# Key norms as two products of 64 rows, and the front of the feed-forward part inside the end of the attention loop

## The chip, the cores and the metric

The kernel runs on one core of one Trainium2 chip. The metric is the device time of one execution in microseconds (us); lower is better. TensorE is called PE here (PEld for its weight loads), VectorE DVE, ScalarE ACT, GpSimd POOL, and the queue that issues the transfers SP.

## The reference

A block of a transformer over 8 sequences of 512 tokens with 256 channels. Cut to what matters:

```python
x = x + _layernorm(attn(_layernorm(x)))          # 16 heads of 64 complex channels
x = x + _layernorm(ffn(_layernorm(x)))           # hidden size 768, silu(gate) * up, int weights / 127

# in attn, for each head (q, k, v are complex, rotated by a phase that depends on the token):
s  = einsum('bihd,bjhd->bhij', qr, conj(kr)).real
qn = (q.real ** 2 + q.imag ** 2).sum(-1)          # norm of each query
kn = (k.real ** 2 + k.imag ** 2).sum(-1)          # norm of each key
maha   = maximum(qn[..., None] + E*E * kn[:, :, None, :] - 2.0 * E * s, 0.0) / V
logits = coef * log1p(maha / nu) - 0.5 * DH * log(V)      # then causal mask and softmax
y      = A @ v                                            # and the output projection Wo
```

E depends on the distance of the two tokens and on the head. The causal mask makes a head's scores a triangle: of four blocks of 128 queries the widest sees 512 keys, then 384, 256 and 128.

## The kernel before

The attention runs as 64 iterations: 8 groups of two heads (the outer loop, `G`), and in each group the 8 sequences (`B`). Iteration t works on the scores and logits of unit t (one sequence, two heads), while it projects and rotates unit t+1 and finishes unit t-1 (its softmax weights are turned and multiplied with the values, and the result goes through the output projection). In `body` of every engine `c` stands for unit t, `cn` for t+1 and `cp` for t-1; `if nxt` and `if old` leave out what has no next or no former unit.

Each engine has its own program, written out by hand, and it takes its instructions strictly in that order. Semaphores tie the engines together: `x.wait_ge(sem, v)` stops an engine (and all that stands behind it) until the count is there. The two PSUM banks `pa` hold projections and norms, `ps` the scores, `pp` turned weights and values, `py` the weighted values, `po` the output projection.

Steps by name, for head `hh` of the unit and block `n` (0 is the widest, 512 columns, 3 the narrowest, 128):

- PE: `project` (6 products of 512 columns), `norm_k` and `norm_q`, `scores`, `turn` (transposes), `attend`, `values`, `out_project`.
- ACT: `square`, `keep_norm_k` (norms of the keys into `kn`), `log`, `exp`, `keep_turned`, `keep_y`, `keep_values`. Log and exp lie in different tables, so ACT loads a table (1.28 us) four times an iteration.
- DVE: `rotate` (8 of them), `decay`, `distance`, `logits`, `bounds`, `inverse`, `add_output` (adds into `acc`).
- POOL: `rotated` (8 of them, 64 x 512), `sum_squares`, `decay_norm` (writes `ek`, which `distance` reads), and once a group `low_weights`.

The squares in `sq` have the 64 channels of head 0 in rows 0 to 63 and those of head 1 in rows 64 to 127. `norm_k` (L710 to 714) multiplies all 128 rows with a matrix `heads[:, hh, :]` that is one in the rows of head hh and zero in the others, and so spreads the norms of one head over 128 partitions; it is called once for each head. All this is 32-bit data, for which one product shows as two MATMUL records.

After the 64 iterations comes the run-out of the last unit, then the feed-forward part, one sequence after the other. For sequence b: `first_norm` (statistics of the attention's sum), `residual` (normalise, add the input, statistics again), `second_move`, `f_normal` on ACT, `f_transposes` on PE, `f_high` and `split_low` (the input as a high and a low part), then six times `gate_up` (PE), `silu` (ACT), `hidden` (DVE, L1577), `hidden_high` (ACT), `hidden_low` (POOL, L635), then `down` (PE), `third_norm`, `third_move`, `f_last` (ACT) and `f_final` (DVE). `f_pow` (POOL, L640) stands between each statistics step and its use. All of the feed-forward part's front for sequence 0 waits for the last `add_output` of the attention: `dve.wait_ge(acc_dve, 4 * B * G + 4)`.

## Time and profile before

| | |
|---|---|
| median of 3 runs | 2025.73 us (2020.53 to 2025.87) |
| the profiled execution | 2020.74 us, its span 2018.9 us |
| busy: PE, DVE, ACT, POOL | 91%, 80%, 78%, 71% of the span |
| share of POOL in the chain that ended last | 49% |

The busy time of PE counts a product until its modelled end, so that a busy PE is not one at its peak. "Idle before" is the time that an engine sat still just before an instruction, with what ended it. The chain that ended last is followed back from the last instruction: it says what released what, not how much slack the other engines had.

### The profile page before, as it was taken

What the parts mean: (1) busy time and instruction counts of PE and PEld (TensorE: products, weight loads), DVE (VectorE), ACT (ScalarE), POOL (GpSimd) and SP (SyncE); (2) the same over time, 40 slices, a digit from 0 to 9 for tenths busy, and PEclk for the clock granted to TensorE, in tenths of its full rate; (3) what the DMA queues carried; (4) which work ended last, traced back from release to release, by engine and by line L of the source; (5) the groups of instructions that cost most, each with busy time, mean ns of one, the idle gap of its engine ahead of it and who ended that gap; (6) DMA issues with size and microseconds to landing.
All of it is one profiled execution on the core that took longest, in us unless ns stands there. A gap on an engine that the chain in (4) does not pass through costs nothing.

```text
span 2018.9 us, 41149 instructions
## 1 busy us (share of the span) xinstructions
PE 1845.1 (91%) x10660; PEld 1512.1 (75%) x10660; DVE 1605.3 (80%) x3834; ACT 1566.9 (78%) x3217; POOL 1440.2 (71%) x1257
## 2 busy tenths in 40 slices
PE   0489999999999999999999999999999999968886
PEld 0358878887878788878787888788888888856665
DVE  5458888888888888888888888888888888865774
ACT  2758888888888888888888888888888888864444
POOL 1377887778777878787778777887778777724443
PEclk9999999999999999999999999999999999999999
DMA  8813111311131113111311131111311110110110
GB/s 178 295 61 105 57 43 43 105 42 37 43 107 42 58 43 105 42 58 43 88 41 58 43 99 49 57 43 56 92 42 43 43 35 33 39 32 11 50 45 32
DMA packets 65069, 128.17 MB, mean 63 GB/s; under 512 B 14448, under 2 KB 44656, under 8 KB 55920
## 3 DMA queue, kind: packets, MB, share of 16 engines
q1 hardware_dynamic: 64880, 126.01, 20.4%
q8 instruction: 75, 1.23, 0.3%
q14 instruction: 114, 0.93, 0.1%
HBM read 107.24 MB, written 25.03 MB: 66 GB/s over the span
## 4 chain that ended last, share of the span: by engine, by line
POOL 49%; issue 23%; PE 12%; DVE 7%; ACT 3%; SPq 2%; POOLq 2%; DMA 1%; ACTq 0%; DVEq 0%
POOL qk L567 27%; POOL ek L576 16%; POOL sq L559 5%; PE pa L705 2%; PE py L766 2%; PE ps L742 2%; PE po L777 2%; DVE stats L1517 1%; PE pp L732 1%; PE pp L754 1%; DVE tabs L1577 1%; POOL rstd L640 1%; PE pa L714 1%; SPq L436 1%; DMA xs_d<-xt 1%
## 5 line engine op out<-in xcount | busy, mean ns | idle before, releaser
L567 POOL TENSOR_TENSOR qk<-rm 64x512 f32<-64x512 f32 x512 | 671.6, 1312 | 83.8 <-DVE rm L1351 23.7
L576 POOL TENSOR_TENSOR ek<-tabs,kn 128x512 f32<-128x512 f32 (+3 forms) x512 | 476.4, 936 | 259.3 <-DVE lg L1376 228.9
L705 PE MATMUL pa<-xt,wt 128*128 128x512 f32 x1536 | 438.2, 421 | 5.0 <-issue 2.6
L1384 DVE CUSTOM_DVE_ANT_0 lg<-lg,tabs,ncog 128x512 f32<-128x512 f32 (+3 forms) x512 | 428.1, 845 | 0.0
L1351 DVE TENSOR_TENSOR rm<-pa,tabs 128x512 f32<-128x512 f32 x512 | 337.6, 680 | 45.0 <-POOL qk L567 36.5
L742 PE MATMUL ps<-qk 128*128 128x512 f32 (+3 forms) x1024 | 351.4, 443 | 20.4 <-DVE lg L1376 18.0
L766 PEld LDWEIGHTS py<-pt,vt 128*128 128x128 f32 x2560 | 343.0, 191 | 27.6 <-ACT pt L1060 4.7
L766 PE MATMUL py<-pt,vt 128*128 128x128 f32 x2560 | 353.7, 276 | 2.5 <-ACT pt L1060 2.1
L1376 DVE CUSTOM_DVE_ANT_0 lg<-ps,ek,qb 128x512 f32<-128x512 f32 (+3 forms) x512 | 278.7, 544 | 75.5 <-DVE ps L1365 57.7
L705 PEld LDWEIGHTS pa<-xt,wt 128*128 128x128 f32 x1536 | 280.4, 189 | 72.4 <-issue 7.4
L1053 ACT ACTIVATE pr<-lg,nmax 128x512 f32<-128x512 f32 (+3 forms) x512 | 285.5, 558 | 56.3 <-DVE nmax L1384 46.7
L1405 DVE SCALAR_TENSOR_TENSOR acc<-po,rden,acc 128x256 f32<-128x256 f32 (+1 forms) x512 | 223.4, 477 | 109.4 <-PE po L777 109.3
L1060 ACT ACTIVATE pt<-pp 128x512 f32<-128x512 f32 (+3 forms) x512 | 212.4, 428 | 123.3 <-PE pp L754 118.1
L777 PE MATMUL po<-wot,yt 128*128 128x256 f32 x1024 | 268.9, 385 | 2.9 <-DVE acc L1405 2.5
L1045 ACT ACTIVATE lg<-lg,qb 128x512 f32<-128x512 f32 (+3 forms) x512 | 264.9, 556 | 6.6 <-DVE ncog L1480 3.4
L1365 DVE TENSOR_TENSOR ps<-ps,tabs 128x512 f32<-128x512 f32 (+3 forms) x512 | 251.2, 491 | 11.5 <-issue 5.5
L754 PEld LDWEIGHTS pp<-ident,pr 128*128 128x128 f32 x1280 | 164.2, 141 | 109.4 <-issue 100.9
L742 PEld LDWEIGHTS ps<-qk 128*128 128x128 f32 x1024 | 171.8, 189 | 98.0 <-DVE lg L1376 52.8
L754 PE MATMUL pp<-ident,pr 128*128 128x128 f32 x1280 | 223.3, 273 | 0.8 <-ACT pt L1060 0.8
L732 PE MATMUL pp<-wt,xt 128*128 128x256 f32 x1536 | 199.3, 286 | 0.0
L777 PEld LDWEIGHTS po<-wot,yt 128*128 128x128 f32 x1024 | 175.0, 190 | 17.5 <-DVE acc L1405 2.2
L732 PEld LDWEIGHTS pp<-wt,xt 128*128 128x128 f32 x1536 | 187.8, 191 | 0.1
(152 smaller groups left out, 2193.4 us busy)
## 6 DMA issues: line engine op xcount, KB each, us to landing
xt<-xs_d SPq DMA_DIRECT2D x62, 1024.0 KB, 4.8
tabs<-vec_d SPq DMA_DIRECT2D x64, 192.0 KB, 4.9
xs_d<-xt SPq DMA_DIRECT2D x8, 1024.0 KB, 5.8
wt<-wraw_d SPq DMA_DIRECT2D x8, 768.0 KB, 7.6
acc<-in_L_attn_x SPq DMA_DIRECT2D x8, 512.0 KB, 7.5
tabs<-rope_d SPq DMA_DIRECT2D x16, 256.0 KB, 5.5
tabs<-in_L_attn_x SPq DMA_DIRECT2D x8, 512.0 KB, 4.6
out<-tabs SPq DMA_DIRECT2D x8, 512.0 KB, 3.0
```

The source lines that it names most:

```text
L567: pool.tensor_tensor(qk[part * DH:(part + 1) * DH, z * HH + hh, :], rm[row, 2 * part, :], rm[row, 2 * part + 1, :], ALU.add if part else A ...
L576: pool.tensor_tensor(ek[:, n % 2, 0:w], tab(par, hh, E2_T, N - w), kn[:, hh, 0:w], ALU.mult).then_inc(ek_pool, 1)
L705: last = mm(pa[r][:, :], wproj(par, z, kt, a, r * P, (r + 1) * P), xt[slot][:, kt, b, :], start=(n == 0), stop=(n == 3 * KT - 1))
L732: last = mm(pp[half][:, jj * W2:(jj + 1) * W2], xt[slot][:, kt, a, j * P:(j + 1) * P], wproj(par, 2, kt, b, 0, W2), start=(n == 0), stop=( ...
L742: mm(ps[n % 2][:, 0:w], qk[:, hh, TILES[n] * P:(TILES[n] + 1) * P], qk[:, HH + hh, 0:w], start=True, stop=True).then_inc(s_rdy, 1)
L754: last = pe.transpose(pp[i][:, j * P:(j + 1) * P], pr[:, hh, o:o + P], ident[:, :])
L766: last = mm(py[:, I * P:(I + 1) * P], vt[:, slot, j, hh * P:(hh + 1) * P], pt[:, i, j * P:(j + 1) * P], start=(j == 0), stop=(j == I))
L777: last = mm(po[:, jj * D:(jj + 1) * D], yt[:, hh, j * P:(j + 1) * P], wot[:, par, hh * D:(hh + 1) * D], start=True, stop=True)
L1053: act.activation(pr[:, hh, at(n)], lg[:, hh, at(n)], ACT.Exp, bias=nmax[:, q:q + 1], scale=-1.0, accum_out=den[:, q:q + 1]).then_inc(ex_ac ...
L1351: tt(rm[:, m, :], pa[r][:, :], ropet(par, m in (IS, RS)), ALU.mult).then_inc(mul_dve, 1)
L1376: dve._custom_dve(bass.dve_ops.TENSOR_ADD_SAT, out=lg[:, hh, at(n)], in0=ps[n % 2][:, 0:w], in1=ek[:, n % 2, 0:w], s0=3e38, s1=qb[:, slot, ...
L1384: dve.tensor_tensor_reduce(lg[:, hh, at(n)], lg[:, hh, at(n)], tab(par, hh, T3_T, N - w), ncog[:, par, 0, hh:hh + 1], 3e38, ALU.add, ALU.m ...
```

## The change

Two things, and an order of all four engines' programs written anew around them.

1. `norm_k`, called twice with 128 rows, becomes `norms_k`, called once: for each head a product of only that head's 64 rows, one directly behind the other. The semaphore `nk_rdy` now counts one per unit.
2. The front of the feed-forward part for sequences 0 and 1 (`first_norm`, `residual`, `second_move`, `f_normal`, `f_transposes`, `f_high`, `split_low` and the first two `gate_up` of sequence 0) moves into the last iteration (`if not nxt`) and into the run-out. For it `f_xin` lies wholly in `tabs[0]`, which the last group does not use, and the transposes of sequence 0 go to `pa` instead of `pp`. SP loads the inputs a group earlier.
3. In the loop `decay`, `distance` and `scores` of blocks 0 to 2 of head 0 are done one iteration earlier, `decay_norm` too, and `sum_squares` stands ahead of `rotated`. In the feed-forward part of the other sequences `residual(b + 1)` moves ahead of `hidden(b, 0)`, `f_final` behind `second_move`, and `split_low` ahead of `third_move`.

```diff
-        f_xin = [seq(0, 0), seq(1, 0)]
-        f_outs = [seq(0, 2), seq(1, 2)]
+        f_xin = [seq(0, 0), seq(0, 2)]
+        f_outs = [seq(1, 0), seq(1, 2)]
...
-            sp.wait_ge(f_dve, 8 * B * G + 8)
-            sp.wait_ge(ek_pool, 8 * B * G + 8)
+            sp.wait_ge(f_dve, 8 * B * (G - 1) + 8)
...
-            def rotated(c, z, hh, part):
+            def rotated(c, z, hh, part, last=False):
...
+                if not last:
+                    pool.wait_ge(rot_pool[hh], c[4] + 2 * z + part + 1)
...
+                pool.wait_ge(rot_pool[1], c[4] + 4)
...
-                decay_norm(c, 0, 2, it.par)
                 decay_norm(c, 0, 3, it.par)
...
-                if nxt:
-                    pool.wait_ge(ek_pool, c[8] + 5)
+                if not nxt:
+                    f_pow(0, 0)
+                if nxt:
+                    sum_squares(cn, 0)
+                    pool.wait_ge(sum_pool, cn[2] + 1)
                     rotated(cn, 0, 0, 0)
                 decay_norm(c, 1, 1, it.par)
                 if nxt:
-                    sum_squares(cn, 0)
+                    pool.wait_ge(ek_pool, c[8] + 6)
+                    rotated(cn, 0, 0, 1)
                 decay_norm(c, 1, 2, it.par)
+                if not nxt:
+                    f_pow(1, 0)
                 if nxt:
                     pool.wait_ge(ek_pool, c[8] + 7)
-                    rotated(cn, 0, 0, 1)
                     rotated(cn, 0, 1, 0)
                     rotated(cn, 0, 1, 1)
                     sum_squares(cn, 1)
-                decay_norm(c, 1, 3, it.par)
-                if nxt:
-                    pool.wait_ge(ek_pool, c[8] + 8)
+                    pool.wait_ge(sum_pool, cn[2] + 2)
                     rotated(cn, 1, 1, 0)
                     rotated(cn, 1, 0, 0)
                     rotated(cn, 1, 0, 1)
-                    rotated(cn, 1, 1, 1)
+                decay_norm(c, 1, 3, it.par)
+                if not nxt:
+                    f_pow(0, 1)
+                if nxt:
                     decay_norm(cn, 0, 0, it.behind)
+                    decay_norm(cn, 0, 1, it.behind)
+                    decay_norm(cn, 0, 2, it.behind)
+                    pool.wait_ge(ek_pool, cn[8] + 3)
+                    rotated(cn, 1, 1, 1, True)
             pool.wait_ge(grp[0], 16 * TABLE_LOADS)
             c0 = counts(pool, 0, PERS)
...
-            def norm_k(c, hh):
+            def norms_k(c):
                 pe.wait_ge(sum_pool, c[2] + 2)
-                pe.wait_ge(mul_dve, c[8] + 7 + hh)
-                mm(pa[hh][:, :], heads[:, hh, :], sq[:, 1, 0, :], start=True, stop=True).then_inc(nk_rdy, 1)
+                pe.wait_ge(mul_dve, c[8] + 8)
+                for hh in range(HH):
+                    row = slice(hh * DH, (hh + 1) * DH)
+                    last = mm(pa[hh][:, :], heads[row, hh, :], sq[row, 1, 0, :], start=True, stop=True)
+                last.then_inc(nk_rdy, 1)
...
                 pe.wait_ge(f_norm, b + 1)
+                dst = pp if b else pa
+                if b == 0:
+                    pe.wait_ge(qb_dve, B * G + 1)
+                    pe.wait_ge(kn_act, 2 * B * G + 2)
+                if b == 1:
+                    pe.wait_ge(pt_act, 8 * B * G + 8)
                 for kt in range(KT):
...
+                if n0 == 0:
+                    pe.wait_ge(x_dve, 8 * B * G + 8)
...
+                if not nxt:
+                    f_transposes(0)
+                if nxt:
+                    norms_k(cn)
+                if old:
+                    out_project(cp, it.before, 1, 0)
+                if nxt:
+                    scores(cn, 0, 0)
+                    norm_q(cn)
+                    scores(cn, 0, 1)
+                if old:
+                    out_project(cp, it.before, 1, 1)
+                turn(c, 0, 1)
+                if nxt:
...
+            turn(c, 1, 3)
+            gate_up(0, 1)
+            out_project(c, 1, 0, 0)
+            attend(c, 1, 1, 1)
+            attend(c, 1, 2, 1)
+            attend(c, 1, 3, 1)
+            out_project(c, 1, 0, 1)
+            out_project(c, 1, 1, 0)
+            out_project(c, 1, 1, 1)
+            gate_up(0, 2)
+            gate_up(0, 3)
+            f_transposes(1)
+            gate_up(0, 4)
+            gate_up(0, 5)
...
+            keep_turned(c, 1, 2)
+            silu(0, 0)
+            keep_turned(c, 1, 3)
+            silu(0, 1)
+            keep_y(c, 1)
+            f_normal(1)
+            hidden_high(0, 0)
+            silu(0, 2)
+            hidden_high(0, 1)
+            silu(0, 3)
...
-                hidden_high(b, 3)
                 if b + 1 < B:
                     f_high(b + 1)
+                hidden_high(b, 3)
                 silu(b, 4)
                 hidden_high(b, 4)
                 silu(b, 5)
                 hidden_high(b, 5)
...
-                distance(c, 0, 1, it.slot)
+                decay(c, 0, 3, it.par)
+                distance(c, 0, 3, it.slot)
+                if old:
+                    logits(cp, 1, 3, it.before)
+                if not nxt:
+                    dve.wait_ge(acc_dve, 4 * (B * G - B + 1) + 4)
+                    first_norm(0)
...
+                    inverse(cp, 0)
+                if nxt:
                     rotate(cn, it.behind, 0, RS)
                     rotate(cn, it.behind, 0, IC)
...
+                    residual(0)
+                decay(c, 1, 2, it.par)
+                if nxt:
+                    rotate(cn, it.behind, 1, RC)
+                distance(c, 1, 2, it.slot)
                 if old:
                     add_output(cp, it.b_before, 0, 0)
-                logits(c, 0, 1, it.par)
-                decay(c, 1, 2, it.par)
-                logits(c, 0, 2, it.par)
-                if nxt:
-                    rotate(cn, it.behind, 1, RC)
+                if nxt:
                     rotate(cn, it.behind, 1, IS)
+                logits(c, 1, 0, it.par)
...
+                if old:
+                    add_output(cp, it.b_before, 0, 1)
+                if not nxt:
+                    first_norm(1)
                 decay(c, 1, 3, it.par)
                 distance(c, 1, 3, it.slot)
...
             c = counts(dve, G * B - 1, PERS)
-            logits(c, 1, 0, 1)
-            logits(c, 1, 1, 1)
-            logits(c, 1, 2, 1)
             logits(c, 1, 3, 1)
             inverse(c, 0)
+            split_low(0)
             add_output(c, B - 1, 0, 0)
             inverse(c, 1)
+            residual(1)
             add_output(c, B - 1, 0, 1)
+            hidden(0, 0)
             add_output(c, B - 1, 1, 0)
             add_output(c, B - 1, 1, 1)
...
+            second_move(1)
             dve.wait_ge(acc_dve, 4 * B * G + 4)
-            first_norm(0)
-            residual(0)
-            second_move(0)
-            first_norm(1)
-            split_low(0)
-            for b in range(B):
+            hidden(0, 1)
+            hidden(0, 2)
+            hidden(0, 3)
+            split_low(1)
+            hidden(0, 4)
+            first_norm(2)
+            hidden(0, 5)
+            for b in range(1, B):
+                if b + 1 < B:
+                    residual(b + 1)
                 hidden(b, 0)
+                if b + 1 < B:
+                    second_move(b + 1)
                 if b >= 2:
                     f_final(b - 2)
-                if b + 1 < B:
-                    residual(b + 1)
                 hidden(b, 1)
-                if b + 1 < B:
-                    second_move(b + 1)
                 hidden(b, 2)
-                if b >= 1:
-                    third_norm(b - 1)
+                third_norm(b - 1)
                 hidden(b, 3)
-                if b >= 1:
-                    third_move(b - 1)
                 if b + 1 < B:
                     split_low(b + 1)
+                third_move(b - 1)
                 hidden(b, 4)
                 if b + 2 < B:
                     first_norm(b + 2)
```

What the diff leaves out: in the loop the order of the other steps on ACT and PE, and the functions of the feed-forward part, which only moved up in the file.

PE, the end of the last iteration but one, in the order of the loop, before (`pp` from `xt` are the values, L714 the key norms, `pp` from `pr` the turns, L721 the query norms, `po` the output projection, `ps` the scores):

```order
L732 MATMUL pp<-wt,xt 128x256 x24
L777 MATMUL po<-wot,yt 128x256 x2
L766 MATMUL py<-pt,vt 128x128
L714 MATMUL pa<-sq,heads 128x512
L754 MATMUL pp<-ident,pr 128x128 x4
L777 MATMUL po<-wot,yt 128x256 x2
L714 MATMUL pa<-sq,heads 128x512
L754 MATMUL pp<-ident,pr 128x128 x3
L721 MATMUL pa<-heads,sq 128x2 x4
L777 MATMUL po<-wot,yt 128x256 x2
L742 MATMUL ps<-qk 128x512
L742 MATMUL ps<-qk 128x384
```

PE, the same place in the changed kernel (L735 the key norms):

```order
L754 MATMUL pp<-wt,xt 128x256 x24
L788 MATMUL py<-pt,vt 128x128
L799 MATMUL po<-wot,yt 128x256 x2
L776 MATMUL pp<-ident,pr 128x128 x4
L735 MATMUL pa<-sq,heads 128x512 x2
L799 MATMUL po<-wot,yt 128x256 x2
L764 MATMUL ps<-qk 128x512
L743 MATMUL pa<-heads,sq 128x2 x4
L764 MATMUL ps<-qk 128x384
L799 MATMUL po<-wot,yt 128x256 x2
L776 MATMUL pp<-ident,pr 128x128 x3
L764 MATMUL ps<-qk 128x256
```

The two products of the key norms now follow each other with nothing between, and scores of three blocks stand behind them, not of two.

DVE, the feed-forward part of one sequence in the middle, before (L1577 is `hidden`, L1563 `f_final`, L1539 the sum in `residual`, L1517 statistics, L1529 the shifts):

```order
L1517 BN_STATS stats<-acc 128x6 x4
L1521 BN_AGGR mv<-stats 128x2 x4
L1524 TENSOR_SCALAR rstd<-mv 128x4
L1577 SCALAR_TENSOR_TENSOR tabs<-ps,tabs 128x512 x2
L1563 TENSOR_TENSOR tabs<-tabs,acc 128x1024
L1529 SCALAR_TENSOR_TENSOR xshift<-mv,rstd 128x4
L1539 SCALAR_TENSOR_TENSOR acc<-acc,rstd,tabs 128x256 x4
L1517 BN_STATS stats<-acc 128x6 x4
L1521 BN_AGGR mv<-stats 128x2 x4
L1524 TENSOR_SCALAR rstd<-mv 128x4
L1577 SCALAR_TENSOR_TENSOR tabs<-ps,tabs 128x512
```

DVE, the same place in the changed kernel (L1521 is `hidden`, L1507 `f_final`, L1483 the sum in `residual`):

```order
L1461 BN_STATS stats<-acc 128x6 x4
L1465 BN_AGGR mv<-stats 128x2 x4
L1468 TENSOR_SCALAR rstd<-mv 128x4
L1521 SCALAR_TENSOR_TENSOR tabs<-ps,tabs 128x512
L1473 SCALAR_TENSOR_TENSOR xshift<-mv,rstd 128x4
L1483 SCALAR_TENSOR_TENSOR acc<-acc,rstd,tabs 128x256 x4
L1461 BN_STATS stats<-acc 128x6 x4
L1465 BN_AGGR mv<-stats 128x2 x4
L1468 TENSOR_SCALAR rstd<-mv 128x4
L1521 SCALAR_TENSOR_TENSOR tabs<-ps,tabs 128x512
L1473 SCALAR_TENSOR_TENSOR xshift<-mv,rstd 128x4
L1507 TENSOR_TENSOR tabs<-tabs,acc 128x1024
```

`residual` of the next sequence moved ahead of `hidden(b, 0)`; before, `hidden(b, 0)` and `f_final` stood in front of it.

DVE, the run-out of the attention, before (L1405 is `add_output`):

```order
L1384 ISA lg,nmax<-lg,tabs,ncog 128x128
L1384 ISA nmax 128x1
L1390 RECIPROCAL rden<-den 128x4
L1405 SCALAR_TENSOR_TENSOR acc<-po,rden,acc 128x256 x2
L1390 RECIPROCAL rden<-den 128x4
L1405 SCALAR_TENSOR_TENSOR acc<-po,rden,acc 128x256 x6
L1517 BN_STATS stats<-acc 128x6 x4
L1521 BN_AGGR mv<-stats 128x2 x4
L1524 TENSOR_SCALAR rstd<-mv 128x4
```

DVE, the run-out in the changed kernel (L1455 is `add_output`, L1513 `split_low`, L1521 `hidden`):

```order
L1440 RECIPROCAL rden<-den 128x4
L1513 TENSOR_TENSOR xt<-pa,xt 128x512 x2
L1455 SCALAR_TENSOR_TENSOR acc<-po,rden,acc 128x256 x2
L1440 RECIPROCAL rden<-den 128x4
L1473 SCALAR_TENSOR_TENSOR xshift<-mv,rstd 128x4
L1483 SCALAR_TENSOR_TENSOR acc<-acc,rstd,tabs 128x256 x4
L1461 BN_STATS stats<-acc 128x6 x4
L1465 BN_AGGR mv<-stats 128x2 x4
L1468 TENSOR_SCALAR rstd<-mv 128x4
L1455 SCALAR_TENSOR_TENSOR acc<-po,rden,acc 128x256 x2
L1521 SCALAR_TENSOR_TENSOR tabs<-ps,tabs 128x512
L1455 SCALAR_TENSOR_TENSOR acc<-po,rden,acc 128x256 x4
```

The whole of `residual(1)` stands between the first and the second `add_output` of the last unit, and `hidden(0, 0)` between the second and the third.

## Rows read from the trace of the kernel before

**Rows 1.** The page: the chain that ended last by engine, and its largest group.

```profile
POOL 49%; issue 23%; PE 12%; DVE 7%; ACT 3%; SPq 2%; POOLq 2%; DMA 1%; ACTq 0%; DVEq 0%
...
L567 POOL TENSOR_TENSOR qk<-rm 64x512 f32<-64x512 f32 x512 | 671.6, 1312 | 83.8 <-DVE rm L1351 23.7
```

**Rows 2.** Busy PE, PEld, DVE, ACT, POOL, clock, DMA: one iteration, then one feed-forward sequence.

```profile
626.00:652.00 26.00, 25.91 (x155) 21.49 (x154) 22.14 (x54) 22.19 (x47) 20.51 (x19) 1.00 0.12 40
1890.00:1914.00 24.00, 19.27 (x108) 15.27 (x107) 16.39 (x45) 11.58 (x24) 10.97 (x9) 1.00 0.14 44
```

**Rows 3.** Who waited for whom, 626 to 652: total, times, longest.

```profile
POOL ek L576 <- DVE lg L1376: 3.9, 3, 1.7
...
PEld ps L742 <- DVE lg L1376: 0.5, 2, 0.3
```

**Rows 4.** PE in order of time: start, length, line, count; the query norms of four iterations.

```profile
139.34 1.02 PE L721 MATMUL pa<-heads,sq 128*128 128x2 f32 x8
...
666.59 0.95 PE L721 MATMUL pa<-heads,sq 128*128 128x2 f32 x8
...
695.51 0.95 PE L721 MATMUL pa<-heads,sq 128*128 128x2 f32 x8
...
1769.20 0.95 PE L721 MATMUL pa<-heads,sq 128*128 128x2 f32 x8
```

**Rows 5.** PE in order of time, around the second product of the key norms.

```profile
639.61 1.02 PE L714 MATMUL pa<-sq,heads 128*128 128x512 f32 x2
640.47 0.49 PE L754 MATMUL pp<-ident,pr 128*128 128x128 f32 x3
640.79 0.95 PE L721 MATMUL pa<-heads,sq 128*128 128x2 f32 x8
```

**Rows 6.** One line, L721: records, shortest, median and longest in ns.

```profile
L721 PE MATMUL pa<-heads,sq x512: 170/251/352, 117.6 to 1769.9; 128*128 128x2 f32 x171
```

**Rows 7.** DVE and PE in order of time, end of attention, feed-forward front.

```profile
1806.71 0.88 DVE L1405 SCALAR_TENSOR_TENSOR acc<-po,rden,acc 128x256 f32<-128x256 f32 x2 [1.22 <-PE po L777]
...
1818.03 1.97 PE L889 MATMUL pp<-ident,tabs 128*128 128x128 f32 x8 [11.35 <-ACT tabs L1161]
1821.50 2.04 PE L903 MATMUL pa<-xt,wgt 128*128 128x512 f32 x4 [1.50 <-DVE xt L1569]
...
1841.53 0.68 DVE L1577 SCALAR_TENSOR_TENSOR tabs<-ps,tabs 128x512 f32<-128x512 f32 x1
...
1862.52 0.68 DVE L1577 SCALAR_TENSOR_TENSOR tabs<-ps,tabs 128x512 f32<-128x512 f32 x1
```

**Rows 8.** DVE, POOL, ACT and PE in order of time, a feed-forward sequence in the middle.

```profile
1886.42 0.68 DVE L1577 SCALAR_TENSOR_TENSOR tabs<-ps,tabs 128x512 f32<-128x512 f32 x1
...
1893.02 1.66 DVE L1539 SCALAR_TENSOR_TENSOR acc<-acc,rstd,tabs 128x256 f32<-128x256 f32 x4
...
1896.81 1.01 POOL L640 TENSOR_TENSOR rstd<-rstd,mhalf 128x4 f32<-128x4 f32 x1 [3.74 <-DVE rstd L1524]
...
1898.06 2.07 ACT L1161 ACTIVATE tabs<-acc,xshift,rstd 128x256 f32<-128x256 f32 x4 [6.59 <-DVE xshift L1529]
...
1889.16 0.74 PE L919 MATMUL py<-wdt,wt 128*128 128x256 f32 x4 [0.80 <-POOL wt L635]
...
1896.86 1.09 PE L903 MATMUL pa<-xt,wgt 128*128 128x512 f32 x4
...
1901.77 0.75 DVE L1517 BATCH_NORM_STATS2 stats<-py 128x6 f32<-128x256 f32 x2
...
1903.82 0.68 DVE L1577 SCALAR_TENSOR_TENSOR tabs<-ps,tabs 128x512 f32<-128x512 f32 x1
...
1910.30 0.68 DVE L1577 SCALAR_TENSOR_TENSOR tabs<-ps,tabs 128x512 f32<-128x512 f32 x1
```

**Rows 9.** DVE in order of time: `logits` of 256 columns at two places of an iteration.

```profile
632.72 1.16 DVE L1384 CUSTOM_DVE_ANT_0 lg<-lg,tabs,ncog 128x256 f32<-128x256 f32 x1
...
648.32 0.47 DVE L1384 CUSTOM_DVE_ANT_0 lg<-lg,tabs,ncog 128x256 f32<-128x256 f32 x1
```

592 lines of the change are left out of this document (291 added, 301 removed).

## The prediction

> **What bounds the kernel now.** I read the page first. It seems to say POOL: the chain that ended last runs through POOL for 49% of the span, and PE, though busy for 91% of the span, takes only 12% of it [rows 1]. But that chain only says who released whom. So I cut out one iteration in the middle (626 to 652 us) and looked at the busy time of each engine: PE 25.91 of 26.00, ACT 22.19, DVE 22.14, POOL 20.51 [rows 2]. Only PE is full. The waits of the same stretch agree: POOL sat 3.9 us waiting for DVE, while PE's weight loads waited only 0.5 us [rows 3]. A busy PE is not yet a PE at its peak, so I looked at how closely its work is packed. The second product of the key norms starts at 639.61 and the turns behind it at 640.47, those at 640.79 give way to the query norms [rows 5]: each begins where the last one's stream ends. The iteration is bound by PE's stream; it repeats from one query norm to the next in 25.80 us (640.79 to 666.59) [rows 4, 5]. The iteration of a group in which POOL splits weights takes 28.92 (666.59 to 695.51), and over all 62 steps from 139.34 to 1769.20 the mean is 26.29 [rows 4].
>
> Behind the loop another limit holds. The last `add_output` ends at 1807.6; PE then idles 11.35 us for the normalised input and 1.50 more for the split, and its first gate products run at 1821.50 in 2.04 us where later ones take 1.09 [rows 7, 8]: the pause has cost it the clock too. `hidden(0, 5)` ends at 1842.2, 34.6 us behind the last sum, `hidden(1, 5)` at 1863.2 [rows 7]. From then on a sequence takes 23.88 us (1886.42 to 1910.30) in which no engine is full: PE 19.27, DVE 16.39, ACT 11.58 of 24.00 [rows 2, 8]. That is a chain of latencies across engines.
>
> **Key norms.** Two records of 512 columns take 0.86 us (639.61 to 640.47), so 0.43 each, and the two heads 1.72 us an iteration [rows 5]. A product of 64 rows is no shorter: it streams the same 512 columns. A gain comes only if products in different rows of the array run side by side. The four records come in the order A1 A2 B1 B2 (A is head 0). A2 needs A's rows again, B1 doesn't: at best A2 and B1 run together, three slots of 0.43 in place of four, 0.43 us saved. If each head's two passes paired with the other's (A1 with B1, A2 with B2), it would be 0.86. The trace of before has no product on 64 rows, so it shows neither. The bound below: nothing overlaps, and the array must run empty before it changes between 128 and 64 rows and once more behind it. The shortest record, a product of 2 columns, takes 170 ns [rows 6]; streaming 2 columns is next to nothing of that, so I take it as the price of one emptying, and lose 0.34 us. So the term is between +0.34 and -0.86; I take -0.43, since it follows from the order of the records with no further condition. Over 63 iterations: 27 us less, and 21 more to 54 less at the bounds.
>
> The Trainium skill bears on both ends. "TensorE: Matmul & The Clock Gate", Part 3, says that products in different row groups start about 4 ns apart and run concurrently; by it the 27 us come. "TensorEngine Tiling (Array Packing)", Key Properties, says that changing the tiling mode drains the array, which speaks against this change; by it some of the gain is given back each iteration. No row here shows either.
>
> **The loop's new order.** Since PE is full, a new order can gain at most PE's waits, 0.5 us, and I count nothing for it. It can lose. I laid the steps of the new order on PE's stream, with 25.37 us for an iteration, and asked for each step who must be done before it. The tightest places are these. `scores(cn, 0, 2)` ends PE's iteration and needs `distance` of block 0, one `decay`, `bounds` and one `distance` after `scores(cn, 0, 0)`: about 0.7 us to spare. `turn(cp, 1, 3)` needs `exp` of block 3 of head 1, which comes behind a table load of 1.28: 0.7 to spare. `rotate(cn, 1, RC)` waits for `rotated` of head 1, which now must wait for `scores(c, 1, 3)`; DVE sits there, and ends its rotations 1.2 us before the key norms want them. `decay_norm(c, 0, 3)` now stands behind the last `rotated` at the iteration's edge, and is done 0.6 us before `distance`. POOL's program has the same 8 rotations, 8 `decay_norm` and 2 sums, 20.51 us, DVE's and ACT's the same work as before [rows 2]: 3 us of room in each. The weight split (28.92 in place of 25.80) stays at the start of POOL's iteration, and `decay_norm` of blocks 3 and 4 wait for it where blocks 1 to 3 did: no change.
>
> **The front inside the end.** Before, 34.6 us lie between the last sum and `hidden(0, 5)`. Now at the last sum the normalised input, both parts of it, two `gate_up` and `hidden(0, 0)` of sequence 0 are done. What is late next is sequence 1: `second_move(1)` stands on DVE behind the last `add_output`, and ACT, which takes its program in order, has `f_normal(1)` ahead of `hidden_high(0, 0)`. So from the last sum on, the time is that from a `f_normal` to a `hidden(b, 5)`: 1898.06 to 1910.98, 12.9 us, less 2.05 for the third statistics (1901.77 to 1903.82), which sequence 0 hasn't [rows 8], plus 0.2 for `second_move`: 11.1. That is 23.5 less. But the last sum is itself later, since the new work lies in the way: two `gate_up` on PE ahead of `out_project(1, 0, 0)` (four groups of 1.09 less the tail of 0.17 that the next one hides, 3.7 [rows 6, 8]), the transposes of sequence 0 (1.0, and about 1.8 waiting for ACT's `f_normal(0)`, itself behind DVE's `residual(0)`), and `residual(1)` between the first and second `add_output`, 3.8 (1893.02 to 1896.81 [rows 8]). Sum 10.3, of which it fills about 1.4 in which PE waited anyway: 8.9 later. Net 14.6 us. SP's loads are no obstacle: they wait for counts of the group before.
>
> **The later sequences.** Count from the end of `hidden(b-1, 5)` (1887.10). Before: `hidden(b, 0)`, `f_final` and `residual` bring POOL's power at 1896.81, which takes 1.01, ACT's `f_normal` starts at 1898.06 and holds ACT for 2.07, and only behind it come `hidden_high(b, 1)`, `silu(b, 2)` and `hidden(b, 2)`, so the third statistics start at 1901.77, 14.7 us behind [rows 8]. Now `residual` starts at once: 3.8, power 1.0, `f_normal` done by +7.5. The third statistics then wait for PE: `down` starts at 1889.16 (+2.1), two `down` and the `gate_up` between them end at 1896.86 (+9.8), and I take +10.0 [rows 8]. Before it, 9.2 us follow to the end of `hidden(b, 5)` (1901.77 to 1910.98) [rows 8]; these are left as they are. New period 19.2 in place of 23.88, 4.7 less, for five sequences 23.4. Sequence 1 had no `f_final` to wait for and took 21.0 (1842.2 to 1863.2): 1.8 less. Sequence 7 has no `residual`: nothing. Sum 25.2. The cover here is PE's own `down`: even if POOL's `hidden_low(b-1, 5)`, which now runs beside `residual`, held it up for 2 us, `f_normal` would end at +9.5, still under 10.
>
> **Sum.** 27 + 14.6 + 25.2 = 66.8 us. The profiled execution took 2020.74 (span 2018.9): 1954 by this sum. It is the lower end of the three runs shown (2020.53 to 2025.87), the median is 5 higher: 1959. I say 1957.
>
> **Rivals.**
> (1) The norms don't gain: no overlap, or the array's emptying eats it (three slots and 0.34 of emptying leave 0.09 us an iteration, 6 in all; four slots lose up to 21). The key norms' start-to-start would stay at 1.6 to 2.0 us. For it: nothing in the trace shows an overlap. The 40 us behind the loop remain: 1979 to 2000, with 1984 for no effect. The page on tiling, above, is the rule that would do this.
> (2) Full pairing, 0.86: 54 + 40 us, 1929. Against it: the records of one head stand behind each other.
> (3) Slower: the loop changes hands to the chain DVE, POOL, PE. From `scores(c, 1, 3)` POOL does five rotations of 1.31 and a sum, about 8 us [rows 1], PE the scores, 1 us, then DVE somewhat over half of its 22.14 [rows 2], `decay`, `distance`, `logits` and `rotate`, until `distance(c, 1, 1)` lets the next `scores(c, 1, 3)` go: some 22 us, with hand-overs 23. A `logits` of 256 columns took 1.16 us at one place and 0.47 at another; the long one ran beside POOL's work [rows 9]. If such losses of 0.7 us hit four more of DVE's steps, the period would pass 25.8, and at 26.5 it eats the 40 us of the feed-forward part: 63 x 0.7 = 44, so 2025 and above. It decides from 1.1 us of new stall per iteration on.
> (4) The feed-forward part gives half: `residual(1)` and the transposes block the end more, or `hidden_high` comes later than laid out: 20 in place of 40 us, 1977 with the norms' gain.
>
> **Chances.** Forecast as summed (1943 to 1972) 0.5; (1) 0.2; (2) 0.1; (4) 0.1; (3) or anything else that takes all of it 0.1. The likeliest is 1957. For 8 in 10 I leave out the upper part of (1) and all of (3): 1928 to 1990. A measurement here tells about 0.3% (6 us) from no change. Faster by over 0.3%: 0.9; within: 0.03; slower: 0.07.
>
> **What would show it.** Key norms: the first record of `norms_k` to the next instruction's start in 1.3 us, not 1.7, with one record starting while the other still runs. Loop: query norm to query norm in 25.4, PE still above 25.2 busy of it, and no wait of PE over 0.5. End: last `add_output` to `hidden(0, 5)` in 11, no pause of PE over 3 us, the first gate products in 1.1. Later: `hidden(b, 5)` every 19.2. It is wrong if a product of 64 rows brings stalls of its own, or if PE starts to wait for DVE in the loop.

## The result, and the profile after

| | median us | runs |
|---|---|---|
| before | 2024.38 | 2020.53 to 2025.87 |
| changed | 1975.59 | 1970.88 to 1978.42 |

The ratio is 0.976, with a 95% interval of 0.9735 to 0.9784: 49 us faster, where 67 were forecast. The profiled execution of the changed kernel took 1975.62 us (span 1973.8). Its trace can be cut at the same marks as that of before. The query norm L743 (formerly L721) marks the iterations, in order of time on PE; columns are start, length, line, count:

```profile
147.47 0.95 PE L743 MATMUL pa<-heads,sq 128*128 128x2 f32 x8
...
668.25 0.95 PE L743 MATMUL pa<-heads,sq 128*128 128x2 f32 x8
...
698.47 0.95 PE L743 MATMUL pa<-heads,sq 128*128 128x2 f32 x8
```

The first one in the loop is 8.1 us later than before (139.34, [rows 4]). Of this, 5.1 come with the order (in `order_only`, below, it is at 144.46), for the other 3.0 see the last section. The last starts at 1759.21, so 62 steps took 1611.7 us, 18.1 less than before. An ordinary step takes 25.12 (643.13 to 668.25, for one), where it took 25.80 and I expected 25.37; one that splits weights takes 30.22 (above, 668.25 to 698.47), where it took 28.92 [rows 4] and I expected no more. The busy times of the stretch of [rows 2], and of one feed-forward sequence:

```profile
626.00:652.00 26.00, 26.00 (x157) 21.16 (x156) 22.95 (x56) 22.90 (x48) 21.36 (x20) 1.00 0.11 40
...
1861.80:1880.74 18.94, 17.92 (x106) 15.39 (x104) 16.23 (x45) 11.55 (x22) 11.85 (x10) 1.00 0.19 56
```

PE is full in the loop as before, and now nearly full in the feed-forward part too. The key norms, on PE in order of time; the last two rows are the same four records seen through narrower windows, two that start at 1731.22 and two at 1731.73:

```profile
1730.60 0.60 PE L776 MATMUL pp<-ident,pr 128*128 128x128 f32 x4
1731.22 1.13 PE L735 MATMUL pa<-sq,heads 64*128 64x512 f32 x4
1732.28 1.13 PE L799 MATMUL po<-wot,yt 128*128 128x256 f32 x4
...
1731.22 0.70 PE L735 MATMUL pa<-sq,heads 64*128 64x512 f32 x2
...
1731.73 0.62 PE L735 MATMUL pa<-sq,heads 64*128 64x512 f32 x2
```

Four records from first start to next instruction: 1.06 us. By [rows 5] they took 0.86 twice. The end, on DVE and ACT:

```profile
1802.38 0.88 DVE L1455 SCALAR_TENSOR_TENSOR acc<-po,rden,acc 128x256 f32<-128x256 f32 x2 [9.16 <-PE po L799]
...
1812.14 0.88 DVE L1455 SCALAR_TENSOR_TENSOR acc<-po,rden,acc 128x256 f32<-128x256 f32 x2 [2.17 <-PE po L799]
...
1813.12 2.08 ACT L1111 ACTIVATE tabs<-acc,xshift,rstd 128x256 f32<-128x256 f32 x4 [8.56 <-DVE xshift L1473]
...
1823.26 0.68 DVE L1521 SCALAR_TENSOR_TENSOR tabs<-ps,tabs 128x512 f32<-128x512 f32 x1
...
1842.19 0.68 DVE L1521 SCALAR_TENSOR_TENSOR tabs<-ps,tabs 128x512 f32<-128x512 f32 x1
```

From the last `add_output` (ends 1813.0) to the end of `hidden(0, 5)` (1823.9) it is 10.9 us, against 34.6 in [rows 7]; but from the last query norm of the loop to that last sum it is 53.8, against 38.4. Later sequences follow each other every 18.9 us, against 23.9 in [rows 8].

What stands behind the last query norm of the loop takes 214.6 us instead of 249.7: 35 less, where 40 were forecast. The loop, where 27 us were forecast from the norms, gave 18 in its 62 steps, but 8 had been lost ahead of them: 10 in all. Together this is 45, the difference of the two spans. The experiments take the change apart. All were timed beside the kernel before, whose median lay between 2024.7 and 2025.9 in them.

### The profile page after: what moved, and what is told of

It is laid out like the page before. It is cut to its first block and busy times, and to the rows that moved or that the text cites. A ratio compares the mean times of both kernels' runs of the same rounds, so it can differ in the third digit from the quotient of the medians.

```text
span 1973.8 us, 41342 instructions
## 1 busy us (share of the span) xinstructions
PE 1815.5 (92%) x10660; PEld 1491.2 (76%) x10660; DVE 1601.2 (81%) x3834; ACT 1577.3 (80%) x3217; POOL 1460.0 (74%) x1257
## 5 line engine op out<-in xcount | busy, mean ns | idle before, releaser
L567 POOL TENSOR_TENSOR qk<-rm 64x512 f32<-64x512 f32 x512 | 693.7, 1355 | 110.9 <-PE ps L764 50.0
L577 POOL TENSOR_TENSOR ek<-tabs,kn 128x512 f32<-128x512 f32 (+3 forms) x512 | 462.8, 910 | 145.1 <-DVE lg L1426 100.3
L1434 DVE CUSTOM_DVE_ANT_0 lg<-lg,tabs,ncog 128x512 f32<-128x512 f32 (+3 forms) x512 | 437.0, 872 | 0.0
L764 PE MATMUL ps<-qk 128*128 128x512 f32 (+3 forms) x1024 | 375.7, 451 | 8.9 <-DVE lg L1426 6.2
L788 PEld LDWEIGHTS py<-pt,vt 128*128 128x128 f32 x2560 | 333.8, 193 | 17.0 <-issue 0.3
L724 PEld LDWEIGHTS pa<-xt,wt 128*128 128x128 f32 x1536 | 287.5, 195 | 71.9 <-issue 14.1
L1082 ACT ACTIVATE lg<-lg,qb 128x512 f32<-128x512 f32 (+3 forms) x512 | 278.8, 558 | 35.5 <-DVE lg L1426 31.6
L1455 DVE SCALAR_TENSOR_TENSOR acc<-po,rden,acc 128x256 f32<-128x256 f32 (+1 forms) x512 | 221.9, 474 | 19.8 <-PE po L799 18.4
L776 PE MATMUL pp<-ident,pr 128*128 128x128 f32 x1280 | 215.3, 275 | 20.4 <-ACT pt L1097 16.3
L1065 ACT ACTIVATE sq<-pa 128x512 f32<-128x512 f32 x256 | 151.8, 593 | 88.2 <-PE pa L724 88.2
L559 POOL TENSOR_TENSOR sq<-sq 128x512 f32<-128x512 f32 x128 | 164.9, 1288 | 63.9 <-ACT sq L1065 63.8
```

The source lines that it names most:

```text
L567: pool.tensor_tensor(qk[part * DH:(part + 1) * DH, z * HH + hh, :], rm[row, 2 * part, :], rm[row, 2 * part + 1, :], ALU.add if part else A ...
L577: pool.tensor_tensor(ek[:, n % 2, 0:w], tab(par, hh, E2_T, N - w), kn[:, hh, 0:w], ALU.mult).then_inc(ek_pool, 1)
L724: last = mm(pa[r][:, :], wproj(par, z, kt, a, r * P, (r + 1) * P), xt[slot][:, kt, b, :], start=(n == 0), stop=(n == 3 * KT - 1))
L764: mm(ps[n % 2][:, 0:w], qk[:, hh, TILES[n] * P:(TILES[n] + 1) * P], qk[:, HH + hh, 0:w], start=True, stop=True).then_inc(s_rdy, 1)
L776: last = pe.transpose(pp[i][:, j * P:(j + 1) * P], pr[:, hh, o:o + P], ident[:, :])
L788: last = mm(py[:, I * P:(I + 1) * P], vt[:, slot, j, hh * P:(hh + 1) * P], pt[:, i, j * P:(j + 1) * P], start=(j == 0), stop=(j == I))
```

## Experiments

### The norms, in the new order and in the old

`norms_full` undoes the norms alone:

```diff
-                    row = slice(hh * DH, (hh + 1) * DH)
-                    last = mm(pa[hh][:, :], heads[row, hh, :], sq[row, 1, 0, :], start=True, stop=True)
+                    last = mm(pa[hh][:, :], heads[:, hh, :], sq[:, 1, 0, :], start=True, stop=True)
```

> The changed kernel with the key norms back as two products of 128 rows, at the same place. Theory: 0.48 us per iteration come back, 64 times: 2006. Rival (in the new order other engines set the pace as soon as TensorE has slack, so the norms are worth less): 1976 to 1990.

Measured 2010.59 us, ratio to before 0.9934 (0.9918 to 0.9951). The norms are worth 35.0 us in the new order. Its ordinary step is 25.72 us: 0.60 more than 25.12, which is more than my theory's 0.48. PE, in order of time:

```profile
671.56 0.60 PE L775 MATMUL pp<-ident,pr 128*128 128x128 f32 x4
672.05 1.98 PE L734 MATMUL pa<-sq,heads 128*128 128x512 f32 x4
673.87 1.03 PE L798 MATMUL po<-wot,yt 128*128 128x256 f32 x4
```

From the turns to the output product it is 2.31 us here and 1.68 with 64 rows (1730.60 to 1732.28, above). Joined, the four records of 128 rows take 1.82, a little more than 0.86 twice.

`same_rows` lets both heads' products read the same 64 rows:

```diff
-                    row = slice(hh * DH, (hh + 1) * DH)
-                    last = mm(pa[hh][:, :], heads[row, hh, :], sq[row, 1, 0, :], start=True, stop=True)
+                    row = slice(0, DH)
+                    last = mm(pa[hh][:, :], heads[row, 0, :], sq[row, 1, 0, :], start=True, stop=True)
```

> The changed kernel with the second head's norm product reading the first head's 64 rows as well (so the second head's key norms are those of the first). Theory (the gain is two heads in different rows at once): the four records run one after another at 0.43, 1.72 instead of 1.06, plus 0.66 x 64 = 42: 2018. Rival (a product of 64 rows is cheaper by itself): no change, 1976.

Measured 2030.78 us, 1.0022 (1.001 to 1.0035): 55 us slower than the changed kernel, and slower than the norms of 128 rows by 20. The rows, the last three from moments of the same product:

```profile
683.85 0.60 PE L776 MATMUL pp<-ident,pr 128*128 128x128 f32 x4
684.38 1.98 PE L735 MATMUL pa<-sq,heads 64*128 64x512 f32 x4
686.29 1.13 PE L799 MATMUL po<-wot,yt 128*128 128x256 f32 x4
...
684.91 0.59 PE L735 MATMUL pa<-sq,heads 64*128 64x512 f32 x1
...
685.34 0.59 PE L735 MATMUL pa<-sq,heads 64*128 64x512 f32 x1
...
685.77 0.59 PE L735 MATMUL pa<-sq,heads 64*128 64x512 f32 x1
```

Here the records start one after another, 0.43 apart from the second on. With different rows they run two and two. The rival, that a product of 64 rows is cheaper by itself, is out. And the full pairing is there. I had ruled it out by the order A1 A2 B1 B2, which I took from how the products are written. Since records of the same rows don't run together, each pair must hold one record of either head. The rows show also what changing between 128 and 64 rows can cost when nothing is paired: 2.44 us from turns to output product against 2.31, so at most 0.13 (the step is 25.96 against 25.72, 0.24 longer; the other 0.11 I can't place). "TensorEngine Tiling (Array Packing)" of the Trainium skill, Key Properties, says such a change drains the array; the 0.13 agrees with it, and is far less than the 0.34 of my bound.

`norms_alone` is the kernel before with the new norms, both behind the first turn:

```diff
-                if nxt:
-                    norm_k(cn, 0)
                 turn(c, 0, 0)
+                if nxt:
+                    norms_k(cn)
                 if old:
                     out_project(cp, it.before, 1, 0)
-                if nxt:
-                    norm_k(cn, 1)
                 turn(c, 0, 1)
```

> The kernel before with one edit: the key norms as two 64-row products, standing after the first turn. Theory (in the trace of after the four records run in two pairs, 1.06 us from first start to the next work, and about 0.18 is lost ahead of them, against 1.72 before): 0.48 us per iteration, 64 times, so 31 us faster than before, 1994. My prediction's pairing of the middle two records only: 0.43 x 64 = 27, 1997. Rival: in the old order another chain than TensorE's decides, and little of it reaches the end: 2015 to 2025.

Measured 2063.84 us, 1.0195 (1.0178 to 1.0212): slower, by 39 us, which neither theory nor rival expected. An ordinary step grew from 25.80 to 26.44. PE in order of time:

```profile
655.90 1.13 PE L716 MATMUL pa<-sq,heads 64*128 64x512 f32 x4 [1.02 <-DVE rm L1351]
```

The two products go into both buffers `pa`, so `norms_k` waits for the last rotary product, `rotate(cn, 1, IC)`, that reads the second of them. Before, the first norm needed only the one ahead of it, and the turn and an output product lay between. The old DVE order has that last product late. `norms_rotate` moves it, and nothing else:

```diff
                 if nxt:
                     rotate(cn, it.behind, 1, RS)
+                    rotate(cn, it.behind, 1, IC)
                 decay(c, 1, 3, it.par)
                 distance(c, 1, 3, it.slot)
                 if old:
                     add_output(cp, it.b_before, 0, 1)
-                if nxt:
-                    rotate(cn, it.behind, 1, IC)
```

> The kernel with the norms alone (old order, 2063.8 us, an iteration every 26.44, TensorE waits 1.0 there for the last rotary product of VectorE) with that one product moved two steps ahead on VectorE, before the last decay product. Theory: that wait is the whole loss; it goes, and the 0.6 of the shorter norms shows: an iteration every 25.2, 78 us faster, 1986. Rival: the product cannot come much sooner, since it waits for GpSimd's rotation and its halves must be ready, and the iteration stays over 26: 2030 or more.

Measured 2003.74 us, 0.9893 (0.9877 to 0.991): 60 us faster than `norms_alone`. The wait is gone, as the rows show, and the ordinary step is 25.52.

```profile
654.52 0.49 PE L745 MATMUL ps<-qk 128*128 128x128 f32 x2 [0.19 <-DVE lg L1376]
...
661.29 1.13 PE L716 MATMUL pa<-sq,heads 64*128 64x512 f32 x4
```

It lies between theory and rival. In the old order the new norms with this move are worth 22 us, 0.28 a step, and not the 0.6 of the new order. The move with the old norms was not tried, so how much of the 22 it gives by itself is not shown. The 0.19 above is a wait of PE that the stretch [rows 2] does not have; what the other 0.1 is stays open. The norms and the order are not two independent terms: the same change of the norms costs 39 us in the old order, brings 22 together with the moved rotary product, and brings 35 in the new order.

### The order by itself

`order_only` undoes the three other parts at once: norms of 128 rows, `f_transposes(0)`, `gate_up(0, 0)` and their kin behind the attention part, and the old order of sequences 1 to 7. The two products of the norms stay one behind the other.

> The changed kernel with its three other parts undone: norms of 128 rows, the front behind the attention part, the old order of sequences 1 to 7. What is left is the new order of the loop. Theory by the sum of what the others were worth in the new order (35 for the norms and 5.5 for the front, measured; 25 for the later sequences, predicted): 1976 + 65 = 2041, so the order alone costs about 17 us. The trace of after says where: the iteration that splits the weights takes 30 to 31.4 us instead of 28.7, and the first one 5 more. Rival, as the prediction counted it: the order alone is worth nothing, 2024.

Measured 2042.67 us, 1.0091 (1.0074 to 1.0108): the order alone costs 17.5 us. By the two profiled executions, whose spans differ by 19.6 us, the cost lies in three places. The seven steps that split the weights take 30.8 to 31.3 us (before 28.3 to 28.9), 16.4 more in all. The first query norm in the loop comes 5.1 later. The two steps at which the outer loop jumps back (last section) take 62.9 us, before 57.3: 5.6 more. The other 53 steps give 4.3 of it back (an ordinary one is 25.72, before 25.80), and what stands behind the last query norm gives 3.3.

Together the four parts add up: 35.0 for the norms, 5.5 for the front and 25.0 for the later sequences (below), less 17.5, make 48.0; the whole change gave 48.8.

What happens in such a step of the changed kernel, on ACT, POOL and DVE:

```profile
672.73 1.47 ACT L349 ACTIVATE wt<-wt 128x1536 fp32r<-128x1536 f32 x1
...
674.28 3.44 POOL L354 TENSOR_TENSOR wt<-wt 128x1536 fp32r<-128x1536 f32 x1 [1.49 <-ACT wt L349]
677.69 1.67 POOL L577 TENSOR_TENSOR ek<-tabs,kn 128x128 f32<-128x128 f32 x2
...
678.49 0.35 DVE L1426 CUSTOM_DVE_ANT_0 lg<-ps,ek,qb 128x128 f32<-128x128 f32 x1 [4.60 <-POOL ek L577]
```

POOL comes to the split at its iteration's start, waits 1.49 us for ACT's half, works 3.44, and only then makes the decay table of block 3, for which DVE sits idle 4.60 us; and behind DVE wait `log`, the turns and PE. In the kernel before, DVE did not wait for POOL there at all. First `logits(cp, 1, 0)` and `logits(cp, 1, 1)` in an ordinary step, then POOL's split and the same two beside it:

```profile
645.75 0.97 DVE L1384 CUSTOM_DVE_ANT_0 lg<-lg,tabs,ncog 128x512 f32<-128x512 f32 x1
...
646.65 0.61 DVE L1384 CUSTOM_DVE_ANT_0 lg<-lg,tabs,ncog 128x384 f32<-128x384 f32 x1
...
670.57 3.49 POOL L354 TENSOR_TENSOR wt<-wt 128x1536 fp32r<-128x1536 f32 x1 [0.80 <-ACT wt L349]
...
671.60 3.00 DVE L1384 CUSTOM_DVE_ANT_0 lg<-lg,tabs,ncog 128x512 f32<-128x512 f32 x1
...
674.53 1.34 DVE L1384 CUSTOM_DVE_ANT_0 lg<-lg,tabs,ncog 128x384 f32<-128x384 f32 x1
...
675.80 0.62 DVE L1376 CUSTOM_DVE_ANT_0 lg<-ps,ek,qb 128x384 f32<-128x384 f32 x1
```

The two took 2.76 us longer beside the split, most of the 3.1 us that this step lost before, and the `distance` behind them (L1376) then started without a wait. In all seven such steps the wide one took 3.0 to 3.3 us. That POOL's work is what slows them fits the traces, as in [rows 9], but was not tried apart.

`split_spread` cuts POOL's part in four pieces (2, 1, 1 and 2 sixths; the five in what I expected is a miscount) and puts them where POOL waits, in this step and the next, which `it.new == -1` marks. PE needs the weights only in the one after. Three of the four:

```diff
-                if it.raw is not None:
-                    low_weights(pool, 1 - it.par, it.ready)
...
+                if isinstance(it.new, int) and it.new == -1:
+                    low_weights(pool, 1 - it.par, it.ready, 2, 3)
                 if nxt:
                     sum_squares(cn, 0)
...
+                    if it.raw is not None:
+                        low_weights(pool, 1 - it.par, it.ready, 0, 2)
+                    if isinstance(it.new, int) and it.new == -1:
+                        low_weights(pool, 1 - it.par, it.ready, 4, 6)
                     decay_norm(cn, 0, 2, it.behind)
```

> The changed kernel with the weight split on GpSimd cut into 5 pieces that stand behind the work VectorE waits for, in that iteration and the next. Theory: the 4.6 us that VectorE waits for the decay table behind the split goes; the iteration takes about 26.5 instead of 30.7, seven times: 29 us faster, 1947. Rival: it is ScalarE's half of the split (1.5 us at the start of its iteration) that costs, and GpSimd's is hidden: 1976 to 1970.

Measured 1943.75 us, 0.9598 (0.9582 to 0.9614): 31.8 us faster than the changed kernel. The two steps that hold pieces now take 25.3 to 25.9 each. POOL in order of time shows a piece without a wait on either side:

```profile
682.65 1.27 POOL L356 TENSOR_TENSOR wt<-wt 128x512 fp32r<-128x512 f32 x1
683.89 0.73 POOL L581 TENSOR_TENSOR ek<-tabs,kn 128x256 f32<-128x256 f32 x1
```

### The feed-forward part

`front_back` puts the front for sequences 0 and 1 behind the last sum (`f_transposes(0)`, `gate_up(0, 0)` and `gate_up(0, 1)` behind the output products, `f_normal(0)`, `f_high(0)` and the first `silu` behind `keep_y`, the norms, `residual` and `second_move` behind the sums, with the powers on POOL).

> The changed kernel with the front of the feed-forward part for sequences 0 and 1 put back behind the attention part. By the trace of after the front inside the run-out saves 23.7 us behind the last sum and makes the last sum about 15 us later, so about 8 us come back: 1984. By the prediction's terms (23.5 and 8.9) 14.6 come back: 1990. Rival: the added waits of the last iteration eat all of it, 1976 or less.

Measured 1981.06 us, 0.9784 (0.9768 to 0.9801): the front gives 5.5 us. By the two traces, from the last query norm of the loop to the last sum it is 40.6 us with the front behind and 53.8 with it inside, 13.2 later where I forecast 8.9. From there to the end of `hidden(0, 5)` it is 29.7 and 10.9.

`residual_late` takes the old order of sequences 1 to 7 on POOL, ACT and DVE. Its core, on DVE:

```diff
-                if b + 1 < B:
-                    residual(b + 1)
                 hidden(b, 0)
-                if b + 1 < B:
-                    second_move(b + 1)
                 if b >= 2:
                     f_final(b - 2)
+                if b + 1 < B:
+                    residual(b + 1)
                 hidden(b, 1)
+                if b + 1 < B:
+                    second_move(b + 1)
                 hidden(b, 2)
```

> The changed kernel with the old order of sequences 1 to 7 in the feed-forward part (the residual of the next sequence behind the first hidden product and the store, second move behind the second, rstd and split back in their places). Theory: the period of a sequence goes from 18.9 back to 23.9, 25 us slower: 2001. Rival: the pool, vector and scalar parts of the old order matter less behind the new front, under 15 us: 1985.

Measured 2000.62 us, 0.9873 (0.9857 to 0.989): 25.0 us, and `hidden(b, 5)` every 23.9 again.

`residual_early` goes the other way in the run-out:

```diff
             split_low(0)
+            residual(1)
             add_output(c, B - 1, 0, 0)
             inverse(c, 1)
-            residual(1)
+            second_move(1)
             add_output(c, B - 1, 0, 1)
             hidden(0, 0)
             add_output(c, B - 1, 1, 0)
             add_output(c, B - 1, 1, 1)
-            second_move(1)
```

> The changed kernel with the residual of sequence 1 moved ahead of the first sum of the last iteration, into 9.2 us in which VectorE is idle, and its second move behind that sum, so that ScalarE need not wait 8.6 us for it. Theory: TensorE's waits of 3.2 and 2.1 us for the sums shrink by about 3 together: 1972.5, and the last sum comes 3 us sooner. Rival: what ends then is the chain of two products and a sum for each half, and nothing is gained: 1975.6.

Measured 1970.18 us, 0.9735 (0.9719 to 0.9752): 5.4 us faster than the changed kernel. That difference is about what such a measurement can tell, but the traces say the same: from the last query norm to the end of `hidden(0, 5)` it is 59.4 us instead of 64.7. On DVE and ACT:

```profile
1797.32 0.88 DVE L1455 SCALAR_TENSOR_TENSOR acc<-po,rden,acc 128x256 f32<-128x256 f32 x2 [5.45 <-PE po L799]
...
1799.77 0.88 DVE L1455 SCALAR_TENSOR_TENSOR acc<-po,rden,acc 128x256 f32<-128x256 f32 x2 [1.44 <-PE po L799]
...
1804.03 0.88 DVE L1455 SCALAR_TENSOR_TENSOR acc<-po,rden,acc 128x256 f32<-128x256 f32 x2 [1.22 <-PE po L799]
...
1799.39 2.06 ACT L1111 ACTIVATE tabs<-acc,xshift,rstd 128x256 f32<-128x256 f32 x4
```

ACT's 8.56 us in front of `f_normal(1)` is gone. The second sum, which stood behind the residual, now waits 1.44 for PE, and PE waits 1.06 for it and no longer 3.17. That pause had cost PE its clock too: the granted clock was 1.00 from 1803 to 1808 and 0.50 from 1810 to 1812. PE in order of time, the last two output products and the first gate product behind them, and the busy times from 1810 to 1812, in the changed kernel:

```profile
1807.96 1.10 PE L799 MATMUL po<-wot,yt 128*128 128x256 f32 x4 [3.17 <-DVE acc L1455]
1810.03 2.07 PE L799 MATMUL po<-wot,yt 128*128 128x256 f32 x4 [0.97 <-DVE acc L1455]
1811.54 2.01 PE L832 MATMUL pa<-xt,wgt 128*128 128x512 f32 x4
...
1810.00:1812.00 2.00, 1.97 (x5) 1.61 (x6) 0.00 (x0) 0.00 (x0) 0.00 (x0) 0.50 0.00 0
```

and in `residual_early`:

```profile
1802.86 1.13 PE L799 MATMUL po<-wot,yt 128*128 128x256 f32 x4 [0.97 <-DVE acc L1455]
1803.64 1.27 PE L832 MATMUL pa<-xt,wgt 128*128 128x512 f32 x4
```

In the changed kernel the last output product and the gate product ran at the 1.2 GHz level and took 0.94 and 0.74 us longer.

### Together

`both` is `split_spread` with `residual_early`.

> The changed kernel with the spread weight split and the early residual of sequence 1 together. Theory: they lie in different stages and add up, 1975.6 less 31.9 less 5.4: 1938. Rival: the early residual's gain came from elsewhere (a calmer start), and nothing is added: 1943.

Measured 1938.21 us, 0.9566 (0.955 to 0.9582). They add up.

`both_act` also cuts ACT's half of the split into three pieces, ahead of the second `square` of each pair and of `keep_norm_k`:

```diff
-                    high_weights(act, 1 - it.par)
...
+                if it.raw is not None:
+                    high_weights(act, 1 - it.par, 0, 2)
                 if nxt:
                     square(cn, 0, 1)
```

> The same with ScalarE's half of the split cut into three pieces, placed where it waits for TensorE. What is left of the split costs 1.25 us over three iterations, seven times, 9 us. Theory: ScalarE's 1.5 us in one piece is a third to a half of it, 4 us faster than the one with both: 1934. Rival: all that is left is GpSimd's work, no change: 1938.

Measured 1935.59 us, 0.9553 (0.9538 to 0.9569). 2.6 us less than `both` is too little for these runs to tell. The steps say where it would be: six of the seven steps with a split are 0.4 shorter (25.1 or 25.5 for 25.5 or 25.9) and the last one 0.8 longer, 1.7 us in all. Its median is the lowest of all kernels here, 40 us below the changed one.

`transposes_later` moves PE's transposes of sequence 0 in `both` behind `out_project(cp, 1, 1)` and `turn(c, 0, 1)`.

> The kernel with both edits, and TensorE's transposes for sequence 0 behind the two output products and the turn of the last iteration, instead of ahead of them. In the trace of after TensorE waits 2.2 us for the normalised rows there with the output products ready behind it. Theory: 1.5 to 2 us faster, 1936, with the last sum that much sooner. Rival: what ends that stage is ScalarE's and VectorE's chain, no change: 1938.

Measured 1937.21 us, 0.9564 (0.9548 to 0.958). No change that can be told; from the last query norm to the end of `hidden(0, 5)` it is 58.9 us against 59.2. The 2.2 us in which PE waited for the normalised rows were not what ended that stage.

## Why the prediction held, and where it didn't

The measured 1975.6 lies in the range of 1928 to 1990, but above the 1943 to 1972 of the forecast as summed. That it came so near is partly luck: the sum's terms were wrong in both directions.

- **PE bounds the loop.** Right for the ordinary step: PE is 26.00 of 26.00 busy after, and what shortens its stream shows in full in the new order (0.60 of 0.63 us).
- **Key norms, 27 us.** Shown: 35.0. Right in kind, by the wrong pairing. The step that failed reads "it follows from the order of the records": the two heads' records run two and two, which saves 0.76 of 2.44 us, and the change of rows costs at most 0.13 (not 0.34).
- **"The loop's new order. ... I count nothing for it."** This is the step that failed by most: it costs 17.5 us. Ordinary steps are indeed the same (25.72 against 25.80). The clause "and `decay_norm` of blocks 3 and 4 wait for it where blocks 1 to 3 did: no change" is wrong. Before, while POOL sat in the split, DVE had two `logits` of the iteration before in its program ahead of the `distance` that needs POOL; they ran slower beside it, and the step lost 2.9 us. Now the `distance` of block 3 is next in its program and waits, and the step loses 5.6. I had compared the place of the split and not what stands behind it. This is 16.4 us of the cost by the traces; the first iteration and the two steps with the outer loop's jump, which the prediction does not mention, cost 5.1 and 5.6, and 7.6 come back elsewhere. `split_spread` shows the part of the split, and that none of it is needed.
- **Tight places of the ordinary step.** I had named four with 0.6 to 1.2 us to spare; none of them opened in an ordinary step. The one with 0.6, `decay_norm(c, 0, 3)` ahead of its `distance`, is where DVE waited 4.60 us when the split stood ahead of it.
- **Front, 14.6 us.** Measured 5.5. Against the trace of before it is 8.3 from the last query norm to the end of `hidden(0, 5)` (64.7 us instead of 73.0), since `front_back` keeps the new order in its front. From last sum to `hidden(0, 5)`: 10.9, forecast 11.1. The term that was mis-sized is "8.9 later": 13.2 by `front_back`. As `residual_early` shows, the places of `residual(1)` and `second_move(1)` make 3.3 of it (50.5 us to the last sum instead of 53.8), and cost 2.0 more behind it (8.9 instead of 10.9). The pause of PE over 3 us that I said would not be there is there, 3.17, for the second sum, and the clock that it cost is some 0.9 us of the 3.3: the last output product took 2.07 instead of 1.13, and the last sum waited 2.17 for it instead of 1.22.
- **Later sequences, 25.2 us.** Measured 25.0. The period is 18.9 instead of 19.2.
- **Rivals.** Rival (2)'s mechanism, full pairing, is what the chip does; its time of 1929 did not come since the order took 17.5 us back and the front gave 9 less. Rival (3)'s chain DVE, POOL, PE exists, but in seven steps and not in all: it is the split that sets it off. `norms_alone` is a kernel in which a new stall in the loop does decide.
- **The sum.** 27 + 14.6 + 25.2 = 66.8 stood for 35.0 + 5.5 + 25.0 - 17.5 = 48.0. Two errors of 8 and 9 us, up and down, and one of 17.5 that stayed.

## What to carry to other kernels

A reordering that leaves the ordinary iteration as it was can still cost in the rare one: walk each engine's queue through the iterations with extra work, ask what stands right behind that work and who waits for it, and cut it into pieces that fit the waits. A shorter operation that joins two others takes over the later of their waits: before joining, move up what the second one needed. In a run-out, work of the next stage belongs where the engine is idle, ahead of the sum that another engine waits for, and not between two of them.

## What the runs showed of the hardware

The two fp32 products of 64 rows, each of two records, ran pairwise though written head by head: 1.06 us against 1.82 for 128 rows, and 1.91 when both read the same rows.

In the first iteration the shorter norms cost time. Busy times in two stretches (columns as in [rows 2]), first of the changed kernel, then of `norms_full`; the number behind the five engines is the granted clock:

```profile
116.00:122.00 6.00, 4.24 (x13) 2.58 (x12) 0.70 (x1) 2.55 (x3) 4.47 (x4) 0.50 0.00 0
122.00:128.00 6.00, 6.00 (x16) 4.17 (x17) 3.67 (x10) 2.29 (x4) 3.70 (x4) 0.59 0.00 1
```

```profile
116.00:122.00 6.00, 5.92 (x16) 2.60 (x14) 0.94 (x3) 2.55 (x3) 4.84 (x5) 0.61 0.00 0
122.00:128.00 6.00, 4.97 (x20) 3.16 (x18) 4.61 (x10) 3.22 (x6) 4.38 (x5) 1.00 0.00 1
```

PE is at the 1.2 GHz level there, after waits of 3.95 us for DVE and 1.76 for POOL. With the norms of 128 rows it was busy for nearly all of the first stretch and back at 2.4 GHz in the second; with 64 rows the 1.76 us are idle and it stayed at the lower level for most of the second. From the first query norm to the second it took 27.2 us against 24.05. In the new order this stretch took 24.1 in both kernels with norms of 128 rows and 25.3 to 28.9 in the nine with 64; the 25.3 is `residual_early`, whose first iteration is the same as that of the changed kernel. What the clock's part in it is was read from the traces and not tried apart.

The two steps at which the outer loop jumps back (568 us is the first in the changed kernel) hold a pause of PE that ends with nothing it waited for in the profile; from 567.6 to 568.2 no engine works. PE's granted clock is 1.00 from 560 to 564 and 0.50 from 568 to 572:

```profile
568.23 2.92 PE L724 MATMUL pa<-xt,wt 128*128 128x512 f32 x6 [3.60 <-issue]
```

The order of the programs sorts them. In the kernel before, PE's pauses are 1.26 and 1.31 us and its granted clock stays at 1.00 in the first; in `norms_alone` and `norms_rotate`, which keep the old order, they are 1.89 to 2.27; in the eleven kernels of the new order 3.15 to 3.81. The two steps together take 57.3 to 59.4 us in the old order and 60.6 to 63.5 in the new one. What in the order does this, and what sets the length of the pause, stays open.
